# A graph layer on one core: the second layer's weights applied in the tail of the second pass, and the groups behind the fourth pass written out

## The chip, the cores and the metric

The kernel runs on one core of one Trainium2 chip. The metric is the device time of one execution in microseconds (us), as a median of runs. The engines are named as the profile names them: PE (TensorE) with its weight loads PEld, DVE (VectorE), ACT (ScalarE), POOL (GpSimd) and SP (SyncE). A "q" behind a name (ACTq, SPq) is that engine's sequencer, which issues DMAs.

## The reference

There are 6250 nodes with 256 features, and 106250 edges (50000 drawn pairs in both directions and one loop for each node). `xn` is the layer norm of `x`. One layer computes

```python
def _hconv(x, W, b, src, dst, n):
    xt = x @ W
    m = segment_sum(xt[src], dst, n) * Binv[:, None]
    out = segment_sum(m[dst], src, n) * Dinv[:, None]
    return out + b

h = prelu(_hconv(xn, W1, b1, src, dst, n), a)
h = _hconv(h, W2, b2, src, dst, n) + xn
gnn = prelu(h, a)
x = x + gnn + mix(xn)                 # mix: linear attention over all nodes
x = x + ffn(layernorm(x))             # ffn: 8 experts, the best 2 of each node
```

So the edges are summed four times, twice by `dst` and twice by `src`. The weights `W2` act on features and the sums act on nodes, so `W2` may be applied before the third and fourth sum or behind them, with the same result up to rounding.

## The kernel before

**Passes.** Nodes lie in NB = 49 blocks of 128 rows. A pass p (0 to 3) reads the table `tables[p]` in HBM. POOL gathers one chunk of 128 rows for each indirect DMA (`gather_pass`, L598), four chunks to a group, 208 groups. SP turns the landing of a group into `s_arr`. DVE writes one-hot matrices (`one_hots`, L1159), PE multiplies a group's chunks with them (`product_pass`, L1649) for one (group, block) pair at a time, 256 pairs, and DVE adds the result to the block's sum in SBUF (`acc_pass`, L1180). The edges are sorted, and block b is complete after pair `LAST_GROUP + b`, with LAST_GROUP = 207: in the last 49 pairs one block closes with each pair.

**End of a pass.** The blocks go to the next table in eight parts (`PARTS`: six of seven blocks, one of six, one of one). In pass 1, DVE's `biased` divides by the count and adds the bias (L1265), ACT's `negated` takes the Relu of the negative (L783), DVE's `leaky` adds it back (L1258), and ACT issues the store of the part (L737). POOL starts the next pass when all parts have landed (`s_tab`, L635). Pass 1 also carries the attention's products (`kv_body`) up to pair 203. ACT clears the sums of the next pass behind its stores (L717).

**Behind pass 3.** The sums of pass 3 stand in `accs[1]`. They are handled in groups of G = 4 blocks (13 groups, the last of one block), by a loop with register addresses (`by_group`, two groups in a turn, the first and last groups outside). A group q goes through: PE transposes the sums (`turn_sums`, L1749), ACT copies them (`act_first`, L817), PE multiplies with the second weights `w2g` (`second_weights`, L1761), DVE scales by the inverse count and adds the skip rows (L1322, `s_z`), ACT takes the Relu of the negative (`act_second`, L824, `s_d1`), DVE finishes the activation, adds the residual and takes the statistics (L1327 to L1337, `s_v1`), ACT takes a square root (L830), DVE refines it (`dve_norm`, L903 to L1346), ACT normalises (L834, `s_xf`), PE transposes the rows (`turn_rows`, L1749), ACT copies them (`act_third`, L840, `s_xftc`), PE makes the router's logits (L1774, `s_lg`), and DVE takes the best two (`dve_third`, L1351 to L1362). SP loads skip and residual rows (`load`, L484 and L485) and stores the normalised rows (`store`, L490).

The order of the program of ACT within one turn is what the code says:

```python
def act_turn(q, par, ahead, here, behind):
    if here:
        act_second(q, par, here)
    if behind:
        act_third(q - 1, 1 - par, behind)
    if ahead:
        act_first(q + 1, 1 - par, ahead)
    if here:
        act_norm(q, par, here)
```

In front of it, ACT issues the loads of the expert weights (L845) and of the expert biases (L847).

**After that**, rows are sorted by expert, the experts run in a loop (L1817 to L1847), and the results `ye_d` are loaded again, weighted and added (L519, L1483), with YL = 3 buffers, and ACT stores the output (L886).

Of the kernel before, what the change touches and what calls it, by code (L numbers as in the profile page):

```python
# [17 lines left out]
P = 128  # L18
# [30 lines left out]
def gps_layer(nc, x, src, dst, gnn_w1, gnn_b1, gnn_w2, gnn_b2, gnn_a, wqkv, wout, bout,  # L49
# [76 lines left out]
    YL = 3  # L126
# [7 lines left out]
    with ctx:  # L134
# [102 lines left out]
        def column(o, f, c):  # L237

            if o == 0:
# [33 lines left out]
            "xb": ((2, F), f32), "xnb": ((2, F), f32), "rs": ((2, F), f32), "sk": ((2, F), f32)})  # L273
        xt_of = [mx["xt"][:, n, :].rearrange("p (k n) -> p k n", n=P) for n in range(2)]

        negative = [region[:, at:at + R7 * F].rearrange("p (b f) -> p b f", f=F)
                    for at in (0, KT * 2 * INNER + 2 * PAIRS * F)]
# [4 lines left out]
        fr = carve(region, {"w1": ((NE, KT, H), f32), "b2r": ((NE, F), f32), "w2g": ((KT, F), f32),  # L282
# [5 lines left out]
        fg = carve(gbuf_flat, {"gT": ((KT, G * P), f32), "xh": ((2, G * F), f32), "xft": ((KT, G * P), f32)})  # L288
        fo = carve(ohg_flat, {"skip": ((G, F), f32), "resid": ((G, F), f32)})
        skips, resids = [fo["skip"], fr["skip"]], [fo["resid"], fr["resid"]]  # L290
        xh = [fg["xh"][:, n, :].rearrange("p (b f) -> p b f", f=F) for n in range(2)]
        NK = 2 * NB
# [23 lines left out]
        s_edges, s_x, s_w, s_vec = sem("s_edges"), sem("s_x"), sem("s_w"), sem("s_vec")  # L316
# [28 lines left out]
        (s_gt, s_gtc, s_u, s_z, s_v1, s_d1, s_fold, s_shift, s_xf, s_xfd, s_xfree, s_xft, s_xftc, s_lg, s_lgc,  # L345
         s_ei, s_ed, s_ex, s_ecnt, s_etot, s_eoh, s_eused, s_esort, s_iw, s_ready,
         s_it, s_t1e, s_c1, s_up, s_b1, s_ge, s_t2, s_c2, s_dn, s_b2, s_yfreed, s_add, s_od) = [sem(n) for n in (
             "s_gt s_gtc s_u s_z s_v1 s_d1 s_fold s_shift s_xf s_xfd s_xfree s_xft s_xftc s_lg s_lgc "
# [6 lines left out]
        N_CONST = 15  # L355
        MASKS_FROM, MASKS_TO, RANKS_TO, COLUMNS_FROM = 32, 56, 126, 140
        XG0 = 4 * (NAG // AS) * AG * 16
        N_VEC = 4 * 16
        N_FW = 8 * 16
# [22 lines left out]
        def by_group(engine, turn, link=None, links=0):  # L382


            turn(-1, 1, G, 0, 0)
            turn(0, 0, G, G, 0)
            with engine.Fori(0, (NG - 2) // 2) as i:
                if link is not None:
                    link.enter(i, links)
                for q, par in ((i * 2 + 1, 1), (i * 2 + 2, 0)):  # L390
                    turn(q, par, G, G, G)
            if link is not None:
                link.leave((NG - 2) // 2)
            turn(NG - 1, 1, 1, G, G)
            turn(NG, 0, 0, 1, G)
            turn(NG + 1, 1, 0, 0, 1)
# [9 lines left out]
        def _(sp):  # L406
# [10 lines left out]
            sp.dma_start(ln["w1"], gnn_w1.rearrange("(k p) f -> p k f", p=P)).then_inc(s_w, 16)  # L417
# [45 lines left out]
            sp.dma_start(mx["wq"], wqkv[0:INNER, :].rearrange("(q p) c -> p q c", p=P)).then_inc(s_wl, 16)  # L463
            arrivals(1, 0, NAG)
# [5 lines left out]
            sp.dma_start(fr["w2g"], gnn_w2.rearrange("(k p) f -> p k f", p=P)).then_inc(s_fw, 16)  # L470
# [6 lines left out]
            arrivals(3, AS, NAG)  # L477


            def load(q, par, n):  # L480
                if not (isinstance(q, int) and q < 2):
                    sp.wait_ge(s_v1, q * 2 - 3)
                    settle(sp)
                sp.dma_start(skips[par][:, 0:n, :], rows(skip_d, q * G, n)).then_inc(s_fl[par], 16)  # L484
                sp.dma_start(resids[par][:, 0:n, :], rows(resid_d, q * G, n)).then_inc(s_fl[par], 16)  # L485

            def store(q, par, n):
                sp.wait_ge(s_xf, q + 1)
                settle(sp)
                sp.dma_start(rows(xf_d, q * G, n), xh[par][:, 0:n, :]).then_inc(s_xfd, 16)  # L490
# [4 lines left out]
            sp.wait_ge(s_fin, 3 * NP + 1)  # L495

            def sp_turn(q, par, ahead, here, behind):
                if ahead:
                    load(q + 1, 1 - par, ahead)
                if behind:  # L500
                    store(q - 1, 1 - par, behind)

            by_group(sp, sp_turn)
# [20 lines left out]
        def _(pool):  # L524
# [108 lines left out]
            for p in range(1, 4):  # L633
                pool.wait_ge(s_idx, 2)
                pool.wait_ge(s_tab, p * 16 * NP)  # L635
                gather_pass(p)
# [27 lines left out]
        def _(act):  # L664
# [69 lines left out]
            def store_part(p, n):  # L734
                lo, hi = PARTS[n]
                act.wait_ge(s_fin, p * NP + n + 1)
                act.dma_start(rows(tables[p + 1], lo, hi - lo), accs[p % 2][:, lo:hi, 0:F]).then_inc(s_tab, 16)  # L737

            def end_pass(p, part=None):

                for n in range(NP):
                    if part is not None:
                        part(n)
                    store_part(p, n)
                act.wait_ge(s_acc[p], PAIR)
# [32 lines left out]
            def negated(n):  # L778
                act.wait_ge(s_hz, n + 1)
                if n >= 2:  # L780
                    act.wait_ge(s_fin, NP + n - 1)
                lo, hi = PARTS[n]
                A(negative[n % 2][:, 0:hi - lo, :], accs[1][:, lo:hi, 0:F], ACT.Relu, scale=-1.0).then_inc(s_hr, 1)  # L783

            end_pass(1, negated)


# [27 lines left out]
            def act_first(q, par, n):  # L815
# [1056 lines left out]
```

## Time and profile before

| | us |
|---|---|
| median of 3 runs | 5623.76 (5618.03 to 5629.4) |
| the profiled execution | 5630.74 |
| its span | 5629.0 |
| PE busy | 4260.8 (76%) |
| PE weight loads busy | 2960.0 (53%) |
| DVE busy | 2909.8 (52%) |
| ACT busy | 1250.2 (22%) |
| POOL busy | 3793.5 (67%) |

The mean granted clock of PE is 0.881 of full. Busy time is time in which an instruction of the engine runs; register, branch, semaphore and DMA-issuing instructions aren't counted. An idle time is put down to what ended it. Busy shares are averages over stages that have different limits, so each stage is read by itself: the four passes (612.8 to 4857 us by the start of the first and the last gather), the groups behind them, the sorting by expert, the expert loop (about 5102 to 5564 us), and the combination at the end.

### The profile page before, as it was taken

To read this page: it belongs to the slowest core of one execution; us is meant where nothing else is said; L and a number is where in the kernel's file an instruction comes from. 1 tells how busy PE (TensorE), PEld (TensorE's weight loads), DVE (VectorE), ACT (ScalarE), POOL (GpSimd) and SP (SyncE) were. 2 spreads that over 40 slices of the span, in tenths; PEclk is the share of its full clock that TensorE was granted. 3 is DMA by queue.
4 is the path that set the end of the run, shared out by engine and by line. 5 is a ranking of instruction groups with operands and counts; after the bars stand their busy time and mean duration, and the time that the engine had idled before them with its cause. 6 is when DMAs were issued, how large, how long until landed. Compare 5 with 4: busy or idle time off the path is not lost. (4 is left out here: it accounts for less than half of the span.)

```text
span 5629.0 us, 68593 instructions
## 1 busy us (share of the span) xinstructions
PE 4260.8 (76%) x18010; PEld 2960.0 (53%) x18011; DVE 2909.8 (52%) x10132; ACT 1250.2 (22%) x3308; POOL 3793.5 (67%) x3968
## 2 busy tenths in 40 slices
PE   4799899999987777776566666655667666667995
PEld 2555566666665555554444444443444444455663
DVE  8788777777874554544433333333333233374334
ACT  0498655555530000000100000000000000132331
POOL 2777777777767777777677777777777777303442
PEclk8899999999999999997788888888787888778997
DMA  3400233333343333334454554444333333421125
GB/s 128 138 2 2 69 105 105 105 105 105 104 152 112 113 113 112 113 109 126 132 146 142 147 146 143 119 133 144 105 105 105 105 105 105 149 89 44 62 64 172
DMA packets 322987, 616.67 MB, mean 110 GB/s; under 512 B 80022, under 2 KB 199410, under 8 KB 322156
## 3 DMA queue, kind: packets, MB, share of 16 engines
q0 software_dynamic: 182400, 464.97, 28.9%
q1 hardware_dynamic: 66704, 75.75, 4.0%
q10 hardware_dynamic: 73564, 72.10, 3.9%
q8 instruction: 151, 2.47, 0.2%
q14 instruction: 168, 1.38, 0.1%
HBM read 525.54 MB, written 87.00 MB: 109 GB/s over the span
## 5 line engine op out<-in xcount | busy, mean ns | idle before, releaser
L598 POOL DMA_INDIRECT rowset<-table,idx x3324 | 3194.8, 961 | 1050.3 <-issue 1026.8
L1649 PE MATMUL PS<-rowset,ohg 128*128 x8192 | 2338.9, 440 | 1066.9 <-SPq L455 1049.4
L1649 PEld LDWEIGHTS PS<-rowset,ohg 128*128 128x128 f32 x8192 | 1746.9, 220 | 1599.8 <-issue 1308.5
L1180 DVE TENSOR_TENSOR rowset<-rowset,PS 128x257 f32 (+1 forms) x1024 | 430.8, 421 | 1919.5 <-PE PS L1649 1871.5
L1159 DVE TENSOR_SCALAR ohg<-iota,dl 128x128 f32<-128x128 f16 x4096 | 935.1, 308 | 30.6 <-issue 30.5
L1574 PE MATMUL PS<-region 128*128 128x416 f16 x3328 | 624.9, 339 | 0.0
L616 POOL DMA_INDIRECT scattered_d<-rowset x384 | 374.0, 974 | 221.3 <-DVEq L983 97.8
L1574 PEld LDWEIGHTS PS<-region 128*128 128x128 f16 x3328 | 325.6, 98 | 257.6 <-issue 0.5
L699 ACT ACTIVATE region<-region 128x128 f16<-128x128 f16 x832 | 328.7, 395 | 477.8 <-DVE region L1083 477.0
L1082 DVE TENSOR_SCALAR region<-iota_c,region 128x832 f16<-128x832 f16 x832 | 404.5, 486 | 10.1 <-issue 9.8
L700 ACT ACTIVATE region<-region 128x128 f16<-128x128 f16 x832 | 321.0, 386 | 0.0
L1574 PE MATMUL PS<-rowset,region 128*128 128x416 f16 x1792 | 319.6, 340 | 0.0
L717 ACT ACTIVATE rowset<-z 128x1799 f32<-128x1799 f16 x28 | 45.1, 1688 | 1081.9 <-DVE rowset L1202 1078.9
L1574 PEld LDWEIGHTS PS<-rowset,region 128*128 128x128 f16 x1792 | 174.4, 97 | 145.5 <-issue 1.7
L1082 DVE TENSOR_SCALAR rowset<-iota_c,region 128x832 f16<-128x832 f16 x448 | 227.0, 507 | 42.3 <-PE PS L1574 42.0
L660 POOL DMA_INDIRECT ye_d<-rowset,fs x108 | 106.6, 987 | 205.8 <-DVE fs L1451 149.8
L1083 DVE TENSOR_SCALAR region<-iota_h,region 128x128 f16<-128x128 f16 x832 | 222.6, 268 | 0.0
L1823 PE MATMUL PS<-region,ohg 128*128 x436 | 208.6, 601 | 0.0
L1847 PE MATMUL PS<-rowset 128*128 x864 | 204.8, 380 | 0.0
L1847 PEld LDWEIGHTS PS<-rowset 128*128 128x128 f32 x864 | 164.8, 191 | 69.1 <-issue 52.2
L760 ACT ACTIVATE region<-PS 128x1024 f32<-128x1024 f32 x49 | 50.2, 1024 | 657.8 <-PE PS L1686 657.8
L699 ACT ACTIVATE region<-rowset,region 128x128 f16<-128x128 f16 x448 | 176.4, 394 | 40.2 <-DVE rowset L1083 39.1
(327 smaller groups left out, 3118.0 us busy)
## 6 DMA issues: line engine op xcount, KB each, us to landing
rowset<-table,idx POOLq DMA_INDIRECT x3324
table<-rowset ACTq DMA_DIRECT2D x18, 896.0 KB, 4.3
region<-xt_d ACTq DMA_DIRECT2D x98, 128.0 KB, 2.6
region<-ye_d SPq DMA_DIRECT2D x12, 1024.0 KB, 8.3
xpad_d<-rowset SPq DMA_DIRECT2D x1, 6272.0 KB, 19.9
xn_d<-rowset SPq DMA_DIRECT2D x49, 128.0 KB
xt_d<-rowset SPq DMA_DIRECT2D x49, 128.0 KB
table<-rowset SPq DMA_DIRECT2D x49, 128.0 KB
```

Of the source, the lines that this page charges most:

```text
L598: gp.indirect_dma_start(rowset[:, at + c % ring, 0:F], None, tables[p], bass.IndirectOffsetOnAxis(idx[p % 2][:, c:c + 1], 0)).then_inc(s_g ...
L616: gp.indirect_dma_start(scattered_d, bass.IndirectOffsetOnAxis(ln["place"][:, c:c + 1], 0), ln["edge"][:, c:c + 1], None).then_inc(s_sc[h] ...
L699: A(ohv[:, k % RING, 0, :], ohs[o][:, k % RING, :], ACT.Copy, scale=column(o, 2, c))
L700: A(ohv[:, k % RING, 1, :], ohs[o][:, k % RING, :], ACT.Copy, scale=column(o, 3, c)).then_inc(s_ohs[o], 1)
L1082: TS(ohc[o][:, k % RING, :], iota_c[:, 0:NC], column(o, 0, c), None, ALU.is_equal)
L1083: TS(ohs[o][:, k % RING, :], iota_h[:, :], column(o, 1, c), None, ALU.is_equal).then_inc(s_oh[o], 1)
L1159: m = TS(ohg[:, at + j, :], iota_1[:, :], dl[p % 2][:, j, v:v + 1], None, ALU.is_equal)
L1180: TT(a, a, pair_sum(p, v), ALU.add).then_inc(s_acc[p], 1)
L1574: m = MM(PS[:, 2 * f + h, 0:HC], ohv[:, k % RING, f, :], ohc[o][:, k % RING, h * HC:(h + 1) * HC], start=False, stop=False)
L1649: m = MM(pair_sum(p, v), ohg[:, v * AG % RAW + j, :], rowset[:, ds(slot_of[v % U] + j, 1), 0:width(p)].rearrange("p a f -> p (a f)"), star ...
L1823: m = MM(PS[:, 2 + k % 2, :], xT[:, k % 2, kt * P:(kt + 1) * P], fr["w1"][:, ds(e, 1), kt, :].rearrange("p a f -> p (a f)"), start=kt == 0 ...
L1847: m = MM(PS[:, 6 + k % 2, 0:F], fe["hT"][:, k % 2, t * P:(t + 1) * P], fa_["w2"][:, ds(es[k], 1), t, :].rearrange("p a f -> p (a f)"), sta ...
```

## The change

- `w2g` is loaded with the attention's weights ahead of pass 1 and no longer in pass 3.
- In the last 49 pairs of pass 1, block by block: DVE's `activated` divides, adds the bias, waits for ACT's Relu and adds it; PE's `weigh` transposes the block, ACT copies it, PE multiplies it with `w2g` one pair later, ACT copies the result back into the sums and issues the store of this block: 49 stores in place of 8.
- Behind pass 3 the transposes of the sums, their copy and the products are gone. DVE scales the sums in place (`dve_sums`), one group ahead. The loop with register addresses is written out for 13 groups. The Relu has a buffer of its own, `low`, for one group. The order of ACT and DVE is new, `xft` and the PSUM banks of turned rows and logits are double, and the skip and residual rows of group 0 are loaded in pass 3.
- YL, the number of buffers of the combination, is 2 and not 3.

The diff, cut to its core:

```diff
-    YL = 3
+    YL = 2
@@ SP
+            sp.dma_start(mx["w2g"], gnn_w2.rearrange("(k p) f -> p k f", p=P)).then_inc(s_wl, 16)
             arrivals(1, 0, NAG)
...
-            sp.dma_start(fr["w2g"], gnn_w2.rearrange("(k p) f -> p k f", p=P)).then_inc(s_fw, 16)
...
+            load(0)
+            arrivals(3, AS, NAG)
             sp.sem_inc(s_xfree, 2)
+            sp.wait_ge(s_fin, FIN_AT[3] + 1)
+            load(1)
+            for q in range(NG + 1):
+                if q + 2 <= NG:
+                    load(q + 2)
+                store(q)
@@ ACT, end of pass 1
-            end_pass(1, negated)
+            def negated(b):
+                act.wait_ge(s_hz, b + 1)
+                A(low_of[b % 2], accs[1][:, b, 0:F], ACT.Relu, scale=-1.0).then_inc(s_hr, 1)
+
+            def turned_sums(b):
+                act.wait_ge(s_gt, b + 1)
+                A(turned[b % 2], PS[:, b % 2, 0:F], ACT.Copy).then_inc(s_gtc, 1)
+
+            def weighted(b):
+                act.wait_ge(s_u, b + 1)
+                A(accs[1][:, b, 0:F], PS[:, b % 2, F:2 * F], ACT.Copy).then_inc(s_fin, 1)
+                act.wait_ge(s_fin, FIN_AT[1] + b + 1)
+                act.dma_start(rows(tables[2], b), accs[1][:, b:b + 1, 0:F]).then_inc(s_tab, 16)
+
+            for b in range(NB + 2):
+                if b < NB:
+                    negated(b)
+                if 1 <= b <= NB:
+                    turned_sums(b - 1)
+                if b >= 2:
+                    weighted(b - 2)
+            clear_for(1)
@@ ACT, groups
+            def act_low(q):
+                n = blocks_in(q)
                 act.wait_ge(s_z, q + 1)
+                if q:
+                    act.wait_ge(s_v1, (q - 1) * 2 + 1)
+                A(fo["low"][:, 0:n, :], accs[1][:, q * G:q * G + n, 0:F], ACT.Relu, scale=-1.0).then_inc(s_low, 1)
+
+            def act_root(q):
+                n = blocks_in(q)
+                act.wait_ge(s_v1, q * 2 + 1)
+                A(sm["rstd"][:, 1, 0:n], sm["rstd"][:, 0, 0:n], ACT.Sqrt).then_inc(s_d1, 1)
...
+            act_low(0)
+            for q in range(NG + 1):
+                if q < NG:
+                    act_low(q + 1)
+                act_root(q)
+                if q:
+                    act_third(q - 1)
+                act_norm(q)
+            act_third(NG)
@@ DVE, pass 1
+            def activated(n, k, v):
+
+                b = v - LAST_GROUP
+                if n or not 0 <= b < NB:
+                    return
+                dve.wait_ge(s_acc[1], v + 1)
+                link(TS(inv[:, 1, b:b + 1], accs[1][:, b, F:FC], 1.0, None, ALU.max))
+                link(V.reciprocal(inv[:, 1, b:b + 1], inv[:, 1, b:b + 1]))
+                STT(out=accs[1][:, b, 0:F], in0=accs[1][:, b, 0:F], scalar=inv[:, 1, b:b + 1], in1=vecs[:, 0, :],
+                    op0=ALU.mult, op1=ALU.add).then_inc(s_hz, 1)
+                dve.wait_ge(s_hr, b + 1)
+                STT(out=accs[1][:, b, 0:F], in0=low_of[b % 2], scalar=not_a, in1=accs[1][:, b, 0:F],
+                    op0=ALU.mult, op1=ALU.add).then_inc(s_lk, 1)
@@ DVE, groups
+            dve_sums(0)
+            for q in range(NG + 1):
+                if q < NG:
+                    dve_sums(q + 1)
+                dve_second(q)
+                if q:
+                    dve_third(q - 1)
+                dve_norm(q)
+            dve_third(NG)
@@ PE, pass 1
+            def weigh(b):
+
+                if b == 0:
+                    pe.wait_ge(s_gmc, 1)
+                if 0 <= b < NB:
+                    pe.wait_ge(s_lk, b + 1)
+                    if b >= 2:
+                        pe.wait_ge(s_fin, FIN_AT[1] + b - 1)
+                    for kt in range(KT):
+                        m = TR(PS[:, b % 2, kt * P:(kt + 1) * P], accs[1][:, b, kt * P:(kt + 1) * P], ident[:, :])
+                    m.then_inc(s_gt, 1)
+                b -= 1
+                if 0 <= b < NB:
+                    pe.wait_ge(s_gtc, b + 1)
+                    for kt in range(KT):
+                        m = MM(PS[:, b % 2, F:2 * F], turned[b % 2][:, kt * P:(kt + 1) * P], mx["w2g"][:, kt, :],
+                               start=kt == 0, stop=kt == KT - 1)
+                    m.then_inc(s_u, 1)
@@ PE, groups
+            for q in range(NG + 1):
+                turn_rows(q)
+                logits(q)
```

`dve_second` begins with a wait for `s_low`, `dve_third(q)` with one for `s_lg` of q, and PE's `logits(q)` with one for `s_xftc` of q, the copy of `act_third(q)`.

## Rows read from the trace of the kernel before

**Rows 1.** Page, costliest groups: count, busy us, mean ns, idle before and releaser.

```profile
L598 POOL DMA_INDIRECT rowset<-table,idx x3324 | 3194.8, 961 | 1050.3 <-issue 1026.8
```

**Rows 2.** Timeline of POOL, first gather of pass 2: start, us, engine, line, idle before.

```profile
2752.25 0.97 POOL L598 DMA_INDIRECT rowset<-table,idx  x1 [14.06 <-issue]
```

**Rows 3.** Timeline, end of pass 1, DVE and ACT.

```profile
2745.43 1.81 DVE L1258 SCALAR_TENSOR_TENSOR rowset<-region,small,rowset 128x1536 f32<-128x1536 f32 x1
...
2748.06 0.42 ACT L783 ACTIVATE region<-rowset 128x256 f32<-128x256 f32 x1 [3.57 <-DVE rowset L1265]
...
2749.03 0.34 ACTq L737 DMA_DIRECT2D table<-rowset  x1
```

**Rows 4.** Timeline, PE: transposes and products of one group of four blocks.

```profile
4909.69 1.97 PE L1749 MATMUL PS<-ident,rowset 128*128 128x128 f32 x16 [2.49 <-ACT rowset L834]
...
4913.70 3.70 PE L1761 MATMUL PS<-region,rowset 128*128 128x256 f32 x16
```

**Rows 5.** Chain of waits: start, us, what; the products of one pair.

```profile
4196.84 2.00 PE PS L1649 x8
...
4860.37 3.79 PE PS L1649 x8
```

**Rows 6.** Stretches: us, busy (x) of PE, PEld, DVE, ACT, POOL, PEclk, DMA, GB/s.

```profile
2700.00:2738.00 38.00, 23.80 (x79) 17.28 (x79) 14.31 (x44) 1.70 (x1) 29.16 (x30) 0.81 0.43 126
```

**Rows 7.** Timeline, one group in the middle of the loop.

```profile
4910.70 1.23 DVE L1327 SCALAR_TENSOR_TENSOR rowset<-rowset,ohg 128x1024 f32 x1 [1.34 <-ACT rowset L824]
4910.82 1.03 ACT L840 ACTIVATE rowset<-PS 128x1024 f32<-128x1024 f32 x1 [0.15 <-PE PS L1749]
...
4911.90 1.95 PE L1774 MATMUL PS<-region,rowset 128*128 128x8 f32 x16 [0.24 <-ACT rowset L840]
...
4915.36 0.17 DVE L1337 TENSOR_SCALAR fs<-fs 128x4 f32<-128x4 f32 x1
4915.44 0.18 DVE L1351 TENSOR_TENSOR fs<-PS,region 128x32 f32<-128x32 f32 x1
4915.66 0.21 ACT L830 ACTIVATE fs<-fs 128x4 f32<-128x4 f32 x1 [2.90 <-DVE fs L1337]
...
4918.45 0.16 DVE L1346 SCALAR_TENSOR_TENSOR fs<-fs 128x4 f32<-128x4 f32 x1
...
4919.34 1.66 DVE L1322 SCALAR_TENSOR_TENSOR rowset<-PS,inv,region 128x256 f32 x4 [0.72 <-issue]
```

**Rows 8.** Timeline, start of the groups.

```profile
4865.39 14.38 ACTq L847 DMA_DIRECT2D rowset<-b_d  x1
...
4894.29 0.17 DVE L1337 TENSOR_SCALAR fs<-fs 128x4 f32<-128x4 f32 x1
```

**Rows 9.** Timelines, end of the groups, DVE and PE.

```profile
5023.16 0.17 DVE L1337 TENSOR_SCALAR fs<-fs 128x4 f32<-128x4 f32 x1
...
5030.53 0.16 DVE L1337 TENSOR_SCALAR fs<-fs 128x1 f32<-128x1 f32 x1
...
5042.07 0.21 DVE L1377 TENSOR_TENSOR ohg<-fs 128x49 f32<-128x49 f32 x1
...
5031.45 3.58 PE L1774 MATMUL PS<-region,rowset 128*128 128x8 f32 x16 [1.11 <-ACT rowset L840]
```

**Rows 10.** Stretches of the groups, columns as in rows 6.

```profile
5028.00:5036.00 8.00, 5.55 (x24) 5.06 (x24) 2.32 (x11) 1.73 (x4) 0.00 (x0) 0.50 0.19 66
...
4995.00:5007.00 12.00, 7.87 (x54) 6.87 (x53) 8.56 (x36) 5.94 (x9) 0.00 (x0) 1.00 0.39 131
```

**Rows 11.** Combination: chain of waits (three rows), then one stretch.

```profile
5570.27 5.25 DMA region<-ye_d
...
5578.95 6.81 DMA region<-ye_d
...
5624.10 0.49 DVE rowset L1483
...
5586.00:5600.00 14.00, 0.00 (x0) 0.00 (x0) 11.62 (x29) 0.00 (x0) 0.00 (x0) 0.50 1.05 395
```

More of the change, by code:

```diff
@@ L380, in rows, with blocks_in @@
             return d[ds(b * P, n * P), :].rearrange("(b p) f -> p b f", p=P)
[L382 to L396, printed above, removed]
+        def blocks_in(q):
+            return G if q < NG else 1
         def settle(engine):
@@ L476, in _, with load, store @@
             sp.dma_start(b1_rows, ffn_b1).then_inc(s_fw, 16)
[L477 to L487, printed above, removed]
+            def load(q):
+                n = blocks_in(q)
+                if q >= 2:
+                    sp.wait_ge(s_v1, (q - 2) * 2 + 1)
+                sp.dma_start(skips[q % 2][:, 0:n, :], rows(skip_d, q * G, n)).then_inc(s_fl[q % 2], 16)
+                sp.dma_start(resids[q % 2][:, 0:n, :], rows(resid_d, q * G, n)).then_inc(s_fl[q % 2], 16)
+            def store(q):
                 sp.wait_ge(s_xf, q + 1)
-                settle(sp)
-                sp.dma_start(rows(xf_d, q * G, n), xh[par][:, 0:n, :]).then_inc(s_xfd, 16)
+                sp.dma_start(rows(xf_d, q * G, blocks_in(q)), xh[q % 2][:, 0:blocks_in(q), :]).then_inc(s_xfd, 16)
                 sp.wait_ge(s_xfd, (q + 1) * 16)
                 sp.sem_inc(s_xfree, 1)
+            load(0)
+            arrivals(3, AS, NAG)
             sp.sem_inc(s_xfree, 2)
[L495 to L503, printed above, removed]
+            sp.wait_ge(s_fin, FIN_AT[3] + 1)
[4 more added lines that the diff above has]
+                store(q)
             sp.sem_inc(s_yfreed, ER)
@@ L634, in _ @@
                 pool.wait_ge(s_idx, 2)
[L635 removed]
+                pool.wait_ge(s_tab, TAB_AT[p] * 16)
                 gather_pass(p)
@@ L1543, in _ @@
             pe.wait_ge(s_wkvc, 2)
-            pe.wait_ge(s_w, 16)
+            pe.wait_ge(s_vec, N_VEC)
             histogram(1)
@@ L1757, in second_weights, with logits @@
+            def logits(q):
+                pe.wait_ge(s_xftc, q + 1)
                 if q >= 2:
-                    pe.wait_ge(s_z, q - 1)
-                for j in range(n):
+                    pe.wait_ge(s_lgc, q - 1)
+                for j in range(blocks_in(q)):
                     for kt in range(KT):
-                        m = MM(PS[:, 2 + 2 * par + j // 2, (j % 2) * F:(j % 2 + 1) * F], fg["gT"][:, kt, j * P:(j + 1) * P],
-                               fr["w2g"][:, kt, :], start=kt == 0, stop=kt == KT - 1)
@@ L1763, in second_weights @@
[L1763 to L1774 removed]
+                        m = MM(PS[:, q % 2, j * NE:(j + 1) * NE], xft[q % 2][:, kt, j * P:(j + 1) * P],
```

214 lines of the change are left out of this document (73 added, 141 removed).

## Prediction

> **What bounds the kernel now.** I read the page first. One group fills most of it: the indirect gathers of GpSimd (L598), 3324 of them, busy 3194.8 us with 1026.8 us of "issue" between them [rows 1]. That is 1.27 us for each gather, 4222 us for four passes, so through the passes the end is set by GpSimd, and work of the other engines inside a pass is free as long as no ring slot comes late. GpSimd stops only where a pass ends and the next table must land: the timeline of GpSimd has 14.06 us of idle time before the third pass [rows 2]. So two places on the path are touched at the passes: these restarts. Then the timeline after the fourth pass: 4865.4 to 5042.1 us belong to the 13 groups [rows 8, 9], 177 us in which the chain goes from engine to engine and no one is full. Last, the combining stage from 5570 us, where the DMA engines are full [rows 11].
>
> **Part 1, the second weights in the tail of pass 2.** Closing a block costs, per step of the last 49 pairs, DVE two small operations, two 256-wide ones and a wait for ACT's 0.42 us [rows 3], about 2.0 us in all (0.15, 0.16 and twice 0.49 beside it), where the old form did the same work for seven blocks at a time. PE gets 4 transposes and 4 products of 256 columns. A group of four blocks took 1.97 and 3.70 us for these at the higher clock [rows 4], so a block takes 0.5 + 0.9 = 1.4 us, at the lower clock about 1.8 times that (the ratio of 3.58 to 1.95 us for the same 16 products, [rows 4, 9]), 2.6 us. A pair's own product is 2.00 us at the higher and 3.79 us at the lower clock [rows 5]. Pairs come every 4.1 us (831 gathers of 1.27 us over 256 pairs). PE thus needs 3.4 us of 4.1 at the higher clock, 6.4 at the lower, and in the tail the granted clock is 0.81 with PE busy 23.80 of 38 us [rows 6]. It keeps up if the clock rises with the work, which I take; DVE (14.31 of 38 us busy [rows 6]) keeps up. At the very end the chain grows. Before: the last block's bias, ACT's 0.42, DVE's second operation, the store issued at 2749.03, and GpSimd starts 3.22 us later [rows 2, 3]. After: a transpose (0.5 to 0.9), ACT copy (0.4), product (0.9 to 1.7, and the product of the block before it has to be done first), ACT copy (0.4), and four hand-overs: 2.6 to 4.0 us. In exchange the 1.81 us operation on six blocks [rows 3], which stood ahead of the last block, is gone. Net +0.8 to +2.2 us; if PE lags by a pair, up to +5; if the added work lifts the clock, -1. I take +2.
>
> The stores of the table become 49 of 128 KB in place of 8; the same bytes, and only the last one's landing is waited for. ACT's queue holds behind them the clearing of the other sums and the row loads of pass 3, which nobody needs before the first pair, some 8 us after the restart: nothing.
>
> w2g now loads at the start of pass 2, on SP's queue, just ahead of the last stores of the first table. 256 KB more at the 350 to 400 GB/s of a full stretch [rows 11] are 0.7 us if all of it is in front of that store. I take +0.5, bounds 0 and +1. Its load vanishes from pass 4, where nobody waited: 0.
>
> **Part 2, the groups.** Three things change: the transposes, the copy and the products of the second weights leave; the Relu has its own buffer and runs one group ahead; and the order on ACT changes. The last decides. Before, ACT's order in a turn is Relu(q), copy of turned rows(q-1), copy of sums(q+1), square root(q), normalise(q). So the copy at 4910.82 and the 16 logit products at 4911.90 are over before DVE ends its statistics at 4915.53, and DVE goes on at 4915.44 with no wait [rows 7]. After, the order is Relu(q+1), root(q), copy(q-1), normalise(q), and Relu(q+1) waits for s_v1 of group q, because there is one `low` buffer. The copy of q-1 stands behind it, so it can't start before the statistics of q end. And DVE's own next step, `dve_third(q-1)`, waits for the logits that need this copy. What was hidden becomes serial.
>
> A period, from the end of one group's statistics to the next: hand-over 0.12, Relu 0.96 to the next issue (1024 columns, like the copy's 1.03), root 0.17 (4915.66 is its start now, 0.12 after the statistics), copy 1.03, so 2.28; hand-over 0.05, the 16 logit products 1.95 [rows 7] or 3.58 us [rows 9], hand-over 0.07; then top-k and Newton, 4915.44 to 4918.61, 3.1 [rows 7]; sums of group q+2, 0.1 + 1.66; second half of DVE's work, 0.1 + 4.83 (4910.70 to 4915.53, [rows 7]). Sum 14.1 us at the higher clock, 15.75 at the lower. Before: from 4894.46 to 5023.33 are 11 periods, 11.72 each [rows 8, 9].
>
> Which clock? Before, PE is busy 7.87 of 12 us in a middle stretch and granted full clock; at the end, with bursts of 16 small products between waits, it is granted 0.50 (1.2 GHz) at 5.55 of 8 us [rows 10]. After, PE has two bursts a period, 2 x 1.95 of 14 us. That is like the end, so I take the lower: 15.75.
>
> The sum, all ends of the statistics. Start: ACT's queue is blocked by the issue of L847 until 4879.8 [rows 8]; then Relu 1.06 and 4.86, so 4885.7 in place of 4894.5: -8.7. Group 1: 1.4 + Newton 1.2 + 1.8 + 4.9 = 9.2, and its DVE also takes the sums of group 2, whose skip rows are asked for at 4885.7 while the expert weights are still landing; +2 for that wait, bounds 0 and +4. Ten periods: 157.5. So 168.7 against 128.9: +39.8. Group 12 (one block): 6.0 + 3.1 + 0.1 + 2.0 = 11.2 against 7.4 (5023.33 to 5030.69 [rows 9]): +3.8. From there the last rows: normalise, turn 3.6, copy 1.0, logits 3.6, top-k 2.0, Newton 1.1, then the one block's own round 3, and hand-overs: 15.6 against 11.4 (5042.07): +4.2. Together +39.1 us; at the higher clock -8.7 + 23.5 + 2.2 + 0.4 = +17.4. Fewer bytes compete with L847, which may free ACT up to 3 us sooner. The register arithmetic of the loop goes too; between 4915.44 and 4918.61 the operations stand end to end, so I give it nothing.
>
> **Part 3, YL from 3 to 2.** Combining: load of 1 MB, 8 DVE operations (3.38 us), out store. Before, the first step ends at 5578.95 and the last, twelve later, at 5624.6: 3.8 us each, with three loads in flight and the DMA engines full (1.05 [rows 11]). With two buffers load q is asked for when q-2 is added, so two steps take one landing plus 3.4 us. The first load landed in 5.25 us without stores beside it, another in 6.81 [rows 11]. I take 6.0: the twelfth step ends at 5578.9 + 5 x 9.4 + 3.4, the last at 5630.4 in place of 5624.6: +5.8; bounds +2 and +10.
>
> The Trainium skill (DMA: Bandwidth & Descriptors, Anatomy of one DMA) gives a transfer 2.0 us fixed plus its bytes at 436 GB/s; by that a load would be back in 4.4 us (my estimate), and the end would come 2 us earlier than now, 8 us under my term. No load here came back so fast; the fit is for DMAs of GpSimd, these are SP's, and the row decides.
>
> **Total:** 39.1 + 2 + 0.5 + 6 = +47.6 us. On the profiled execution (span 5629.0, time 5630.74) that is 5678.3. It was 7.0 us over the median of the three runs, so from 5623.76: **5671 us**, +0.85%.
>
> **Rivals.** (a) *The same order, but PE at the higher clock*: 17.4 + 8.5 = +26, 5650. For it: the full clock of the middle stretch, which has gaps of some us too. Against: less than half their PE work is left. (b) *DVE never waits for the logits*: the copy gets through in time, the gain of the removed work shows. Then a period is DVE's own work, 3.1 + 0.3 + 1.66 + 4.9 = 9.9 us; ten are 99, and with the start the groups come to -31, the total to -22: **5601**. It decides at the point where the copy of q-1 can be issued before the statistics of q end; for it speaks that DVE is only some 70% busy and PE idle, against it the order in the text of ACT's program, which is served in order everywhere in this trace. (c) *PE falls behind in the tail of pass 2*: if the clock stays at 0.8, a pair and a block need about 4.3 us of 4.1, some 10 us behind after 49 steps, with the growing wait of DVE in it up to 20: about 5686. Against it: DVE's last pairs have no one-hots to make. (d) *Nothing to measure*: DVE waits only in part of the groups, half way between (a) and (b), 5626.
>
> **Chances.** Forecast 0.62, (a) 0.17, (c) 0.11, (b) 0.06, (d) 0.04. Range: down to (a) with the low ends of the landing and of the L847 term, 5650 - 10 = 5640; up to the forecast with its upper bounds (YL +4, tail +3, skip rows +2, others +4), 5684, nearly to (c). A measurement of this kernel can tell about 0.2% (11 us) from no change. Slower 0.89, same 0.05, faster 0.06.
>
> **What would show it.** In the trace after: DVE's logit addition waiting 4 to 6 us for PE in each group; ACT's Relu and root ahead of the copy; statistics ends 14 to 16 us apart; granted clock 0.5 there; first statistics near 4886 (plus the shifts of the passes); GpSimd's gap before pass 3 near 16 us; DVE waiting for DMA 2 to 3 us every second step of the combining. It is wrong if DVE has no wait in front of the logit addition (then (b)), or if the gap before pass 3 grows by 10 us (c).

## The result, and the profile after

The changed kernel takes 5653.25 us (median of 5 runs, 5651.4 to 5659.8) against 5623.76 us before. The ratio is 1.0053 (95% interval 1.0039 to 1.0068): 29.5 us slower. The forecast was 5671 us, with a range of 5640 to 5684.

The profiled execution took 5652.78 us, 22 us more than the profiled one of before, which was itself 7 us above its median. By stage, in us, each taken from the starts and ends of the gathers (L598 before, L587 after) and of the first instruction of the next stage:

| stage | before | after |
|---|---|---|
| gathers of pass 1, first to last | 1053.2 | 1046.6 |
| GpSimd's gap before pass 1, 2, 3 | 14.4, 14.1, 9.5 | 15.9, 12.5, 8.8 |
| gathers of pass 3, to the issue of the bias load | 1051.9 | 1047.8 |
| groups: from that issue to the first step of the sorting | 176.7 | 199.7 |
| sorting and experts | 528.2 | 524.6 |
| combination | 58.7 | 75.0 |

So the loss stands where the forecast had put it, in the groups (+23.0) and in the combination (+16.3), and 17 us of it come back in the passes and the expert stage. Part of that is scatter between executions: a later run whose passes and experts are those of the kernel before (b_yl2, below) has 1047.7 us from the first gather of pass 3 to the bias load and 524.6 us in sorting and experts, as the changed kernel has, and its groups take 183.6 us. Against it the groups of the changed kernel cost 16 us more, not 23.

The groups. Timeline of the changed kernel, two ends of the statistics (L1340) and what lies between: start, us, engine, line, idle before and what ended it. They answer to [rows 7].

```profile
4883.42 0.17 DVE L1340 TENSOR_SCALAR fs<-fs 128x4 f32<-128x4 f32 x1
...
4883.69 1.06 ACT L825 ACTIVATE ohg<-rowset 128x1024 f32<-128x1024 f32 x1 [10.11 <-DVE fs L1340]
...
4884.65 0.19 ACT L830 ACTIVATE fs<-fs 128x4 f32<-128x4 f32 x1
4884.74 1.00 ACT L847 ACTIVATE rowset<-PS 128x1024 f32<-128x1024 f32 x1
4885.80 3.58 PE L1784 MATMUL PS<-region,rowset 128*128 128x8 f32 x16 [10.14 <-ACT rowset L847]
4889.42 0.19 DVE L1355 TENSOR_TENSOR fs<-PS,region 128x32 f32<-128x32 f32 x1 [5.83 <-PE PS L1784]
...
4891.91 0.16 DVE L1349 SCALAR_TENSOR_TENSOR fs<-fs 128x4 f32<-128x4 f32 x1
4891.99 1.67 DVE L1323 SCALAR_TENSOR_TENSOR rowset<-rowset,inv,ohg 128x256 f32<-128x256 f32 x4
...
4893.58 1.22 DVE L1332 SCALAR_TENSOR_TENSOR rowset<-rowset,region 128x1024 f32<-128x1024 f32 x1
...
4898.00 0.17 DVE L1340 TENSOR_SCALAR fs<-fs 128x4 f32<-128x4 f32 x1
```

The reader is to see the one idle time, 5.83 us, in front of DVE's logit addition L1355, where [rows 7] have none. Above it stand its makers in ACT's order: the Relu (L825), the root (L830), then the copy (L847), then PE's 16 products at 3.58 us, all behind the end of the statistics. From 4883.42 to 4898.00 are 14.58 us.

A stretch of the groups shows PE's granted clock (columns as in [rows 6]): PE busy 22.21 of 58 us at 0.50, which is 1.2 GHz.

```profile
4884.00:4942.00 58.00, 22.21 (x96) 20.22 (x96) 33.35 (x144) 16.24 (x28) 0.00 (x0) 0.50 0.34 109
```

The combination, DVE's steps. They answer to [rows 11].

```profile
5613.13 3.38 DVE L1485 SCALAR_TENSOR_TENSOR rowset<-region,ohg,rowset 128x256 f32<-128x256 f32 x8 [3.37 <-DMA region<-ye_d]
5616.88 3.38 DVE L1485 SCALAR_TENSOR_TENSOR rowset<-region,ohg,rowset 128x256 f32<-128x256 f32 x8 [0.37 <-DMA region<-ye_d]
5623.56 3.38 DVE L1485 SCALAR_TENSOR_TENSOR rowset<-region,ohg,rowset 128x256 f32<-128x256 f32 x8 [3.30 <-DMA region<-ye_d]
...
5638.04 3.38 DVE L1485 SCALAR_TENSOR_TENSOR rowset<-region,ohg,rowset 128x256 f32<-128x256 f32 x8 [0.81 <-DMA region<-ye_d]
5645.62 1.01 DVE L1485 SCALAR_TENSOR_TENSOR rowset<-region,ohg,rowset 106x256 f32<-106x256 f32 x2 [4.20 <-DMA region<-ye_d]
```

Two steps take 10.3 to 11.0 us, here 10.4, with a wait of about 3 us in every second one. The first load landed in 5.2 us, the other eleven of 1 MB in 6.9 to 8.0. The last row is the step on the last block: its load of 212 KB was asked for at 5637.26 and came 8.3 us later, and DVE waited 4.20 us for it.

The tail of pass 1. Timeline of the changed kernel: the last store of the table and the restart of GpSimd, answering to [rows 2, 3].

```profile
2741.48 0.39 ACT L779 ACTIVATE rowset<-PS 128x256 f32<-128x256 f32 x1 [0.48 <-PE PS L1725]
2741.90 0.33 ACTq L781 DMA_DIRECT2D table<-rowset  x1
...
2744.33 0.94 POOL L587 DMA_INDIRECT rowset<-table,idx  x1 [12.49 <-issue]
```

The stretch (columns as in [rows 6]):

```profile
2700.00:2732.00 32.00, 23.19 (x107) 18.11 (x106) 16.46 (x56) 7.70 (x24) 24.22 (x25) 0.99 0.47 140
```

With the added work the granted clock of this stretch is 0.99, where it was 0.81 [rows 6], and GpSimd's gap is shorter than before, 12.49 against 14.06 us [rows 2].

### The profile page after: what moved, and what is told of

Read it like the earlier page. It is cut to its first block and busy times, and to the rows that moved or that the text cites. A ratio compares the mean times of both kernels' runs of the same rounds, so it can differ in the third digit from the quotient of the medians.

```text
span 5651.0 us, 68394 instructions
## 1 busy us (share of the span) xinstructions
PE 4239.4 (75%) x18010; PEld 2954.7 (52%) x18011; DVE 2925.8 (52%) x10255; ACT 1269.5 (22%) x3434; POOL 3781.1 (67%) x3968
## 3 DMA queue, kind: packets, MB, share of 16 engines
q8 instruction: 152, 2.49, 0.2%
## 5 line engine op out<-in xcount | busy, mean ns | idle before, releaser
L587 POOL DMA_INDIRECT rowset<-table,idx x3324 | 3185.0, 958 | 1048.8 <-issue 1018.3
L1651 PE MATMUL PS<-rowset,ohg 128*128 x8192 | 2310.5, 436 | 1020.2 <-SPq L447 1003.7
L1651 PEld LDWEIGHTS PS<-rowset,ohg 128*128 128x128 f32 x8192 | 1729.5, 217 | 1536.2 <-issue 1254.4
```

The source lines that it names most:

```text
L587: gp.indirect_dma_start(rowset[:, at + c % ring, 0:F], None, tables[p], bass.IndirectOffsetOnAxis(idx[p % 2][:, c:c + 1], 0)).then_inc(s_g ...
L1651: m = MM(pair_sum(p, v), ohg[:, v * AG % RAW + j, :], rowset[:, ds(slot_of[v % U] + j, 1), 0:width(p)].rearrange("p a f -> p (a f)"), star ...
```

## The experiments

Chips differ for this kernel, and the numbers can't be read without knowing it. On chips 0 and 8 the kernel before takes 5621.6 and 5623.3 us, as in the measurement of the result (5623.8). On chips 10 and 1 it takes 6726 and 6742 us. Below, a fast chip is one of the first kind and a slow chip one of the second. Each run is compared with before on its own chip. On the slow ones I read the groups and the combination by stage, since these take nearly the same time there (groups of the changed kernel 199.7 us on its fast chip, 200.0 and 199.9 on the slow ones).

**The order on ACT.** One edit of the changed kernel, run on a slow chip (a_order) and then on a fast one (a_order_f):

```diff
             for q in range(NG + 1):
+                if q:
+                    act_third(q - 1)
                 if q < NG:
                     act_low(q + 1)
                 act_root(q)
-                if q:
-                    act_third(q - 1)
                 act_norm(q)
```

> The changed kernel with one edit: in ACT's program of the groups, the copy of the turned rows of group q-1 stands ahead of the Relu of q+1 and the root of q, and no longer behind them. Theory (the order puts the copy and the 16 logit products behind the statistics, 5.8 us of DVE waiting in each group): that wait falls to at most 3 us, the ends of the statistics come 9 us (PE at the higher clock) to 11.7 us (lower clock) apart in place of 14.6, the groups take 32 to 60 us less than the 200 us of the changed kernel, and the whole is 32 to 60 us faster than it, so as fast as before or faster. Rival (the groups are slow because PE is at the lower clock): the order changes little, the distance stays at 14 us or more and the time within 10 us of the changed kernel's.

> The changed kernel with the copy of the turned rows ahead of the Relu and the root on ACT, again, for a chip on which PE doesn't wait for its instructions in the passes (chips differ in that, and the first time it was one on which it does). Theory: groups 167 us in place of 200, the whole 29 to 37 us less than the changed kernel's, so within 10 us of before. Rival: what the order gives in the groups is lost elsewhere, and the whole stays at 20 us or more above before.

On the fast chip: 5621.34 us, ratio to before 0.9996 (0.9987 to 1.0005), 32 us less than the changed kernel (the two ratios compared, 0.9996 and 1.0053, since their chips may differ). The groups took 166.3 us in place of 199.7. On the slow chip they took 166.8, but the whole was 1.0061 (1.0038 to 1.0084) of before, 46 us slower, where "as fast as before or faster" had been expected; what is lost there outside the groups is read below, with c_after. Timeline of a_order_f:

```profile
4917.86 0.17 DVE L1340 TENSOR_SCALAR fs<-fs 128x4 f32<-128x4 f32 x1
4917.93 0.18 DVE L1355 TENSOR_TENSOR fs<-PS,region 128x32 f32<-128x32 f32 x1
4918.12 1.06 ACT L825 ACTIVATE ohg<-rowset 128x1024 f32<-128x1024 f32 x1 [3.94 <-DVE fs L1340]
...
4923.57 1.67 DVE L1323 SCALAR_TENSOR_TENSOR rowset<-rowset,inv,region 128x256 f32<-128x256 f32 x4 [2.99 <-DMA region<-resid_d]
```

The 5.83 us are gone: L1355 starts as the statistics end. In their place a new wait of 3 us appears, which I had not expected. The sums now wait for the residual rows of their group, asked for when the statistics of two groups before end (4918.0), which are back only some 5.5 us later. So the distance from one end of the statistics to the next is 11.6 to 11.8 us. I had worked out the same 11.7 for another reason (PE's chain at the lower clock), so the number alone would have misled.

**The clock of PE.** The changed kernel with products that nobody reads:

```diff
             for q in range(NG + 1):
                 turn_rows(q)
+                fill(0)      # 7 products of 512 columns, unused PSUM bank
                 logits(q)
+                fill(1)      # 14
```

> The changed kernel with filler products on PE into an unused PSUM bank in the groups: 7 of 512 columns behind the turning of the rows and 14 behind the logits. Nothing waits for them. Theory (the lower clock of PE adds to each group's serial part what 16 logit products take more, 3.58 against 1.95 us): the granted clock rises from 0.5 to near 1 there, the logit products take 1.95 us, the distance between groups falls from 14.6 to about 13.0 us, and the whole is 15 to 22 us faster than the changed kernel. Rival (the clock doesn't matter, other work sets the distance): no change; if the filler itself gets in the way at the lower clock, slower by up to 20 us.

The groups took 188.7 us on a slow chip, 11 less than without the filler (199.9 in a_yl3 on the same chip, 200.0 in c_after on the other). The whole is 1.0116 (1.0088 to 1.0145) of before there, where c_after has 1.0112 on the other slow chip: the 15 to 22 us expected in the whole did not show, and with such intervals 11 us can't be told from nothing. A stretch of the groups of a_fill (columns as in [rows 6]):

```profile
6060.00:6180.00 120.00, 92.37 (x389) 52.84 (x387) 71.11 (x319) 35.86 (x61) 0.00 (x0) 0.75 0.33 108
```

And its timeline, two rounds of logits:

```profile
6103.77 3.58 PE L1785 MATMUL PS<-region,rowset 128*128 128x8 f32 x16 [3.54 <-ACT rowset L848]
...
6118.36 2.69 PE L1785 MATMUL PS<-region,rowset 128*128 128x8 f32 x16 [2.96 <-ACT rowset L848]
```

The granted clock is 0.75 and not near 1, and the logit products take 3.58 us after 3.54 us of idle time and 2.69 after 2.96, and 2.2 to 3.6 in the ten middle groups, where 1.95 was expected: the filler keeps the clock up only in part. The distances fall from 14.58 to 13.2 to 13.9 us in most groups. So part of the loss is the clock's, by stage about the 11 us recovered here. The order costs more, 33 us.

**The buffers of the combination.** The changed kernel with three (a_yl3), and the kernel before with two (b_yl2, fast chip):

```diff
-    YL = 2
+    YL = 3
```

> The changed kernel with three buffers for the combination in place of two (the semaphore of the bias copy is shared with that of the output to free one). Theory (with two buffers a load of 1 MB takes 7.2 us to land, of which only one DVE step of 3.4 us hides a part): the combination shortens by 16 us, from 75 to 59 us, and so does the whole. Rival (the last stage is longer for another reason, the loads merely met busier DMA engines in that execution): less than 4 us.

> The kernel before with two buffers in the combination in place of three, nothing else. Theory (the buffers alone make the +16 us of the last stage): the combination takes 75 us in place of 59, the whole 14 to 18 us more than before. Rival (something of the changed kernel ahead of it lengthens the last stage): under 4 us.

a_yl3: combination 58.8 us in place of 75 to 77.9, the whole 1.0087 (1.0064 to 1.0109) of before on a slow chip, against 1.0112 for c_after on the other; that is the 16 us by size, but the intervals overlap. b_yl2: combination 74.5 us, the whole 1.0034 (1.0022 to 1.0047), 5640.85 us: +19, where the stage gives +16. In the stage the buffers alone make the difference, in both directions, and b_yl2 shows it in the whole too.

**Slow gathers in the tail of pass 1.** Pass 1 got 6.6 us shorter, which the forecast had not. Two stretches of the timeline of the kernel before, GpSimd and DVE at the same moment:

```profile
2570.75 0.94 POOL L598 DMA_INDIRECT rowset<-table,idx  x1 [0.30 <-issue]
2572.00 2.19 POOL L598 DMA_INDIRECT rowset<-table,idx  x1 [0.31 <-issue]
```

```profile
2571.28 2.08 DVE L1258 SCALAR_TENSOR_TENSOR rowset<-region,small,rowset 128x1792 f32<-128x1792 f32 x1
```

The gather that starts inside DVE's operation over seven blocks takes 2.19 us. All six of these operations have such a gather (1.71 to 2.29 us), and b_yl2 has six again (1.71 to 2.33 us); the changed kernel, with 49 operations of 0.49 us, has none over 1.18 us. The experiment is the kernel before with

```diff
-                STT(out=part(1, n), in0=negative[n % 2][:, 0:PARTS[n][1] - PARTS[n][0], :], scalar=not_a, in1=part(1, n), ...)
+                for b in range(lo, hi):
+                    m = STT(out=accs[1][:, b, 0:F], in0=negative[n % 2][:, b - lo, :], scalar=not_a, in1=accs[1][:, b, 0:F], ...)
+                m.then_inc(s_fin, 1)
```

> The kernel before with one edit: in the tail of pass 1, DVE's second activation step over seven blocks (one operation of 2.08 us) is made block by block, seven operations of about 0.42 us. Theory (a gather whose issue on GpSimd falls on a long two-input operation of DVE on SBUF takes up to 2.3 us in place of 0.95, and this is where pass 1 of the changed kernel won 6.6 us): no gather of that tail over 1.3 us, their mean from 1014 to about 975 ns, the pass 5 to 7 us shorter and the whole as much faster than before. Rival (the 6.6 us are scatter between executions): the same slow gathers, no change in the time.

> The kernel before with the second activation step of pass 1 block by block, again. Where gathers go at 1.27 us: pass 1 5 to 7 us shorter and the whole as much faster than before. On a chip where the gathers wait for ring slots anyway: no gather of pass 1 over 1.3 us, but no gain.

> The kernel before with the second activation step of pass 1 block by block, again, for a chip on which PE doesn't wait for its instructions in the passes. Theory: no gather of the tail of pass 1 over 1.3 us, pass 1 5 to 7 us shorter, the whole 4 to 8 us less than before. Rival: the gathers are as in theory but GpSimd gives the time back elsewhere, the whole within 2 us of before.

Groups of gathers in the tail on fast chips (count, busy us, mean ns), first the kernel before, then b_split_f:

```profile
L598 POOL DMA_INDIRECT rowset<-table,idx x136 | 137.9, 1014 | 41.5 <-issue 39.0 <-DVE rowset L1180 2.4
```

```profile
L598 POOL DMA_INDIRECT rowset<-table,idx x134 | 130.9, 977 | 40.8 <-issue 38.4 <-DVE rowset L1180 2.4
```

In all three runs no gather of pass 1 takes over 1.3 us, and on the fast chip pass 1 takes 1047.1 us against 1053.2 and (b_yl2) 1052.3. So it is shown that the long gathers go with the long operation: of the six profiled executions on fast chips the two with it have six each, the four with pieces none (b_unroll, with the long operation on a slow chip, has three). That they make up the 5 to 6 us of the pass rests on one execution with the split against two without. In the whole the 4 to 8 us expected are not seen: b_split_f is 5621.51 us, ratio 0.9996 (0.9987 to 1.0005), which reaches from 7 us less to 3 us more. On the slow chips the ratios are 1.0015 (0.9999 to 1.0030) and 1.0016 (1.0003 to 1.0029): no gain.

**The loop written out**, alone, in the kernel before:

```diff
-            with engine.Fori(0, (NG - 2) // 2) as i:
-                ...
-                for q, par in ((i * 2 + 1, 1), (i * 2 + 2, 0)):
-                    turn(q, par, G, G, G)
+            for q in range(1, NG - 1):
+                turn(q, q % 2, G, G, G)
```

> The kernel before with one edit: the loop over the groups is written out, nothing else moves. Theory: the register arithmetic between DVE's operations goes, 0.5 to 1 us in each of 11 groups, the groups take 166 to 172 us in place of 177, the whole 5 to 11 us less. Rival: it costs nothing now (0 us), or the longer program costs fetches (up to +5 us).

Ratio 1.0004 (0.9989 to 1.0018), on a slow chip; groups 184.0 us against 180.6 and 181.9 with the loop on such chips. The expected 5 to 11 us did not come. Most distances of the statistics were 10.8 to 11.4 us, against 11.3 to 11.7 in the loop (b_split2), but four of the eleven were 14.2 to 15.4 us. The timeline shows what a long one is made of:

```profile
6042.03 3.70 PE L1756 MATMUL PS<-region,rowset 128*128 128x256 f32 x16
...
6055.87 6.44 PE L1756 MATMUL PS<-region,rowset 128*128 128x256 f32 x16
...
6062.35 1.66 DVE L1317 SCALAR_TENSOR_TENSOR rowset<-PS,inv,region 128x256 f32<-128x256 f32 x4 [3.42 <-PE PS L1756]
```

The stretch (columns as in [rows 6]):

```profile
6050.00:6066.00 16.00, 14.06 (x62) 12.59 (x60) 9.25 (x37) 6.19 (x10) 0.00 (x0) 0.64 0.40 132
```

The 16 products of the second weights take 6.44 us in place of 3.70, at a granted clock of 0.64 in the stretch, and DVE's sums wait 3.42 us for them. Each of the four long distances has such a wait (3.0 to 3.7 us). The kernel before has them too, with the loop:

```profile
4961.64 6.20 PE L1761 MATMUL PS<-region,rowset 128*128 128x256 f32 x16
...
4968.23 1.66 DVE L1322 SCALAR_TENSOR_TENSOR rowset<-PS,inv,region 128x256 f32 x4 [3.21 <-PE PS L1761]
```

There are two such groups in the execution read for the forecast (2.3 and 3.2 us of waiting) and four in b_yl2 and in b_split_f, whose groups took 183.6 and 182.0 us against 176.7. So this is what scatters in the groups of before, and what ate the gain of the unrolled loop: about 0.5 us in an ordinary group, lost in four long ones, of which b_split2 on the same chip has three (14.1 to 14.6 us). Why the clock falls in some groups and not in others is open.

**The changed kernel on a slow chip**, and a version with the faults mended:

> The changed kernel itself, beside the others on one chip. On a chip whose gathers go at 1.27 us each it is 24 to 38 us slower than before. On a chip whose gathers go slower (a pass of 1210 to 1330 us) the groups and the combination cost the same +23 and +16 us; theory: the tail of pass 1 with its 49 stores in the queues of the gathers adds some 25 us there, so about +65 to +80 us. Rival: the excess there belongs to the moved order or to the third buffer, and the changed kernel alone is at +30.

6825.38 us, ratio 1.0112 (1.0092 to 1.0132), 84 us over before: a little above the +65 to +80 of the theory, far from the rival's +30, and more than its groups and combination explain. By stage against b_split2 and b_unroll on the same chip: groups +16 to +18, combination +18 to +19, pass 1 +11 to +15 (1283.6 us), the gap before pass 2 62.0 us against 42.4 and 43.5, +19. The gap is 60.4 to 63.1 us in all five runs with the changed tail on slow chips and 42.4 to 45.6 in the three without. The waits of PE tell what is different on these chips; first the changed kernel on its fast chip, then c_after (waited for, us in total, times, longest):

```profile
PE PS L1651 <- SPq L447: 1003.7, 460, 16.6
```

```profile
PE PS L1651 <- issue: 1303.9, 800, 3.6
```

On the fast chip PE waits in the passes for arrived gathers. On the slow one it stands idle 800 times, 1304 us, for nothing that the profile shows, where the fast chip has 1.5 us of that. The expert stage, a loop, takes 525 us on both. Late instructions would explain it, since the passes are straight-line code, and the expectations of the later runs speak as if it were so ("PE waits for its instructions"), but no run isolates that. The profile's queue of instruction transfers moved 152 packets in both executions, so the 800 idle times of c_after don't stand one to a packet either. What is shown is that PE stands idle more in each pair there, and that the changed kernel, with 8 more products and transposes in each of 49 steps, loses another 31 to 33 us in that tail and the gap behind it.

best2 mends four things in the changed kernel. On ACT the copy comes first, then the root, then the Relu; `YL = 3`, with the shared semaphore of a_yl3; and:

```diff
-                if q:
-                    dve_third(q - 1)
                 dve_norm(q)
+                if q:
+                    dve_third(q - 1)
...
-                    TT(part(p, n), part(p, n), inv[:, 0, lo:hi].unsqueeze(2).broadcast_to([P, hi - lo, F]),
-                       ALU.mult).then_inc(s_fin, 1)
+                    for b in range(lo, hi):
+                        m = TS(accs[p % 2][:, b, 0:F], accs[p % 2][:, b, 0:F], inv[:, 0, b:b + 1], None, ALU.mult)
+                    m.then_inc(s_fin, 1)
```

> The changed kernel with four edits: on ACT the copy of the turned rows first, then the root, then the Relu; on DVE the refinement of the root ahead of the top-k; three buffers in the combination; and the means of passes 0 and 2 block by block. Theory: no group waits for the logits, the ends of the statistics come 9 to 10 us apart, groups about 145 us, combination 59 us, 3 to 5 us less in each of passes 0 and 2: 75 to 90 us faster than the changed kernel, 45 to 60 us faster than before where gathers go at 1.27 us. Rival (PE at the lower clock binds the chain of turning, copy and logits): 11.7 us apart, groups 167 us, 50 to 60 us faster than the changed kernel.

Slow chip: ratio 1.0031 (1.0016 to 1.0047), 58 us under c_after, where 75 to 90 were expected. The groups took 159.4 us, the distance was still 11.6 to 11.9 (once 12.5): by its number the rival. But its timeline has DVE waiting 2.4 to 3.3 us for residual rows in each of these groups, as in a_order_f. best3 takes that wait away and leaves PE as it is (the core of the edit):

```diff
-                if q >= 2:
-                    sp.wait_ge(s_v1, (q - 2) * 2 + 1)
+                if q >= 2:
+                    sp.wait_ge(s_z, q - 1)
                 sp.dma_start(skips[q % 2][:, 0:n, :], rows(skip_d, q * G, n)).then_inc(s_fl[q % 2], 16)
-                sp.dma_start(resids[q % 2][:, 0:n, :], rows(resid_d, q * G, n)).then_inc(s_fl[q % 2], 16)
+
...
+            def load_resid(q):      # waits for s_v1 as before, counts on another semaphore (s_lnd), for which dve_second waits
...
+            load(2)                 # ahead of the loop, in which load(q + 3) follows load_resid(q + 2)
```

> The changed kernel with the four edits of best2 and a fifth: the skip rows of a group are asked for when the sums that used their buffer are done, the residual rows apart from them as before, so that DVE doesn't wait for them. Theory (DVE's own work sets the distance now): 9.2 to 10 us from one end of the statistics to the next, groups 135 to 142 us, the whole 15 to 24 us faster than best2. It is faster than before by 10 to 60 us, less where PE waits for its instructions in the passes. Rival (PE at the lower clock binds the chain of turning, copy and logits): 11.6 us apart as in best2, no gain over it.

Fast chip: **5557.95 us, ratio 0.9886 (0.9871 to 0.9902)**, 64 us faster than before on the same chip (60 had been expected at most) and 95 under the 5653.25 us of the changed kernel. Its timeline, one period of the groups:

```profile
4894.47 0.17 DVE L1352 TENSOR_SCALAR fs<-fs 128x4 f32<-128x4 f32 x1
...
4897.54 1.67 DVE L1334 SCALAR_TENSOR_TENSOR rowset<-rowset,inv,region 128x256 f32<-128x256 f32 x4
...
4901.40 3.59 PE L1796 MATMUL PS<-region,rowset 128*128 128x8 f32 x16 [1.11 <-ACT rowset L857]
...
4903.56 0.17 DVE L1352 TENSOR_SCALAR fs<-fs 128x4 f32<-128x4 f32 x1
```

The stretch around it (columns as in [rows 6]):

```profile
4880.00:4940.00 60.00, 37.58 (x163) 34.20 (x163) 55.42 (x230) 26.64 (x44) 0.00 (x0) 0.50 0.51 173
```

The distance is 9.1 us, groups 130.7 us (both below the 9.2 and 135 expected at the least), and DVE is busy 55.42 of 60 us. PE is still at 0.50 with products of 3.59 us: the lower clock costs DVE no wait once the products lie beside its work. That settles the rival of best2. The pieces of the means shortened pass 0 to 1051.1 us, but GpSimd's gap behind it grew to 18.4 us from 15.9 in the changed kernel, so some 2.5 of the 6 us go back; behind pass 2 the gap stayed (8.7 against 8.8).

## Why the prediction was right, and where its terms were off

**The mechanism was the one forecast.** The copy behind the statistics, DVE's wait for the logits (5.83 us; "4 to 6"), the lower clock (0.50) and the distances ("14 to 16 us apart": 14.6) are there, and moving two lines on ACT takes 33 us of the groups away. Rival (b) falls with the wait of L1355. Rival (d) falls too, since DVE waits in every group: nine of the ten middle distances are 14.58 us. Rival (a), which gave 5650 and lies nearest to the time, is not what happened: its clock was wrong, and its number agrees by chance.

**The groups: +23.0 and not +39.1.** Start -11.9 (forecast -8.7): the issue of the bias load blocked ACT 11.48 us in place of 14.38. That fewer bytes compete with it, which the forecast allowed for outside its sum, is argued and not isolated. The wait for the first skip rows was 5.9 us and not 2, +3.4 in that distance. The largest error lies in the ten periods, 144.6 us where I had 157.5. An ordinary one takes 14.58 us where I had 15.75:

| from one end of the statistics to the next, us | forecast | after |
|---|---|---|
| to the start of DVE's logit addition | 5.98 | 5.83 |
| top-k and Newton | 3.1 | 2.65 |
| sums | 1.76 | 1.59 |
| second half of DVE's work | 4.93 | 4.51 |

The tenth is 13.40, because it takes the sums of one block and not of four. I had read 3.1 and 4.83 us off [rows 7] and had given the removed register arithmetic nothing because the operations "stand end to end". They do not quite: the small operations start 0.20 us apart before as after, but between groups of them there were gaps of 0.1 to 0.2 us, which I took for part of the operations and which are gone in the written-out form. The last two steps came to +2.2 each, forecast +3.8 and +4.2. The side before was read too smoothly as well: its 11.72 us a period are a mean over a first one of 9.9, ordinary ones of 11.2 to 11.7 and two of 14.6 and 13.2, in which DVE waited for the second weights' products at a lower clock. The forecast's stretch of before with a granted clock of 1.00 [rows 10] lies behind these.

**The combination: +16.3 and not +5.8, outside its bounds of 2 and 10.** Two things failed. The first is the landing of a load: I set 6.0 us between 5.25 and 6.81, as if fewer loads in flight must land sooner. The loads on which the pace hangs took 6.9 to 7.6 us, medians of all 7.2 here and 7.3 in b_yl2, against 8.3 with three in flight. With 7.2 my own formula, two steps in a landing plus 3.4 us, gives 10.6 us; measured 10.5 in the mean. So the 6.81 us of before was a fair guide to the steady state, and the 5.25 of the first load, with no stores beside it, was not. This made the twelfth step 6.4 us later than my formula. The second is the last step. I let it end 1.1 us behind the twelfth, but its small load is asked for when the eleventh is done and took 8.3 us, so that DVE waited 4.20 us for it: 4.1 us more. The sum had nothing for this, though before DVE had waited 2.49 us at the same place. 6.4 and 4.1 are the 10.5 us. The Trainium skill (DMA: Bandwidth & Descriptors, Anatomy of one DMA) would have given 4.4 us by my estimate from its figures; no load of 1 MB in these runs landed in under 4.8, and those beside the stores took 6.7 and more, so the rows decide against that figure for these transfers.

**The tail of pass 1: -1.6 in the gap, forecast +2; and -6.6 in the gathers, forecast nothing.** PE's clock did rise with the work, as assumed, so rival (c) falls on this chip; for the gap the forecast had named this case ("-1") and yet taken +2. On the slow chips, where c_after loses some 30 us there, (c) is near to what happens. The gain in the gathers was missed: I had counted DVE's work by its sum and not asked what length of operation GpSimd meets. The w2g load ahead of pass 1 cost up to +1.4 us (15.9 against 14.4; forecast +0.5), but b_yl2 and b_split_f without it have 14.7.

**The sum.** The term of the groups was 16 us too high (39.1 against 23.0) and that of the combination 10.5 us too low (5.8 against 16.3). That these two offset each other in part is luck, and the total owes its nearness to it. The gain in the gathers had no term. The kernel before scatters in its groups too: 176.7 us in the execution read for the forecast, 182.0 and 183.6 in two later ones on fast chips. The forecast of +47.6 against +29.5 has the sign and the place right, and its size is 60% too large.

## What to carry to other kernels

When a step is moved ahead of another on an in-order engine, look for who waits for the step that is now behind it: here the place of one copy in ACT's program made a hidden chain of copy and products serial, for 33 us. A wait removed shows the next one, so read the timeline of each repaired version before its number is taken for a theory's. A buffer taken away from a stage that is near its DMA limit is priced with a landing measured beside the same stores, not with a value nearer to the best one seen, and the last load is followed to its end by itself.

## What the runs showed of the hardware that I had not expected

A gather issued by GpSimd takes 0.95 us, and 1.7 to 2.3 us where it falls on a two-input DVE operation of 2.08 us on SBUF; with DVE's operations of 0.42 to 0.49 us the longest was 1.18 to 1.28 us. Splitting such operations shortened pass 1 by 5 to 6 us in the traces. Passes 0 and 2 of best3, with their means in pieces, took 1051.1 and 1044.4 us against 1057.7 and 1051.7.

In the groups of the kernel before PE's granted clock is not steady: the same 16 products take 3.70 us in some groups and up to 6.7 in others, and in two to four groups of an execution DVE waits 2.1 to 3.7 us for them.

The same program takes 5622 us on some chips and 6726 to 6742 us on others. There PE is idle in the passes for nothing that the profile shows, 1304 us in c_after. The changed kernel costs 30 us on one kind and 84 on the other.
